# A state-space block with an expert block on one core: four kinds of scratch arrays in memory, laid out with the partition outermost

## The chip, the cores and the metric

The kernel runs on one core of a Trainium2 chip. The core has TensorE (PE in the rows), VectorE (DVE), ScalarE (ACT), GpSimd (POOL) and SyncE (SP), which run side by side and meet at semaphores, and 16 DMA engines that move data between the on-chip memory of 128 partitions and the large memory. The metric is the device time of the whole kernel in microseconds (us), as the median of several runs. Lower is better.

## The reference

The input x has 4 sequences of 1024 tokens with 128 features. First a selective state-space block:

```
xn = layernorm(x);  xi, z = split(xn @ W_in)          # 256 channels each
u  = silu(causal_conv4(xi));  dt, B, C = split(u @ W_xproj)   # 8, 64, 64 wide
delta = softplus(dt @ W_dt + b_dt);  A = -exp(A_log)
for t:  h = h * exp(delta_t * A) + (delta_t * u_t) * B_t;   y_t = h . C_t    # 256 x 64 states
x = layernorm(x + x + (y + u * D) * silu(z) @ W_out)
```

then four layers with four experts each (router, top 2 of 4, layernorm, gelu between two matrices of 128x512 and 512x128), a residual and a last layernorm.

## The kernel before

The kernel has three stages.

**The front** (to about 195 us) computes everything of the state-space block that does not depend on the state. It works on 8 items, k = 0 to 7: item k is half a sequence pair, that is 512 tokens (TT) of one of the two sequences (bb = k % 2) of index it = k // 2. For each item PE, ACT and DVE make u, the gate silu(z) (called sz), C, delta, delta*u and B. Delta, delta*u and B are then split into bf16 parts (the value, its rounding rest, and the rest of that), so that products of parts give fp32 accuracy; six pairs of parts (PAIRS) are used, and for each pair one copy of the delta part, the delta*u part and the B part is stored. All of it goes to scratch arrays in the large memory: `dl_d` (delta, six copies), `du_d` (delta*u, six), `b_d` (B, six), `u_d` and `sz_d` (u and the gate, fp32) and `c_d` (C).

**The scan** (about 170 to 1300 us) works on chunks of 64 tokens (TC); a chunk of a sequence pair is two blocks of 128 channels (kk = 0, 1), 64 blocks in all. A block needs the rows of its chunk in another arrangement than the front made them: `load_args` reads `dl_d` with 8 DMAs of 24 KB into `rhs_d[kk]`, `load_products` reads `b_d` with one DMA of 192 KB and `du_d` with 8 of 24 KB into `Bst[kk]` and `rhs_u[kk]`, `load_c` reads `c_d`, and `load_post` reads `u_d` and `sz_d`. PE multiplies them (L1227 the arguments of the exponential, L1240 the products delta*u*B), ACT takes them out of PSUM (L977 with the exponential, L989), DVE runs the recurrence (`tensor_tensor_scan`, L1596, eight a block), and PE sums the states with C (L1257).

**The experts** (about 1300 us to the end) run on PE above all (L1360, L1372).

All stores of the front and all loads of the scan are issued by SP, one after another in program order. In the front its loop over k does, in this order: load the input of item k + 3 (L516); store u and sz of item k (L593, waits for `a_sz`, `a_u`); in the last item (LAST, k = 7) `load_products(0, 0, 0)` for the first block, once POOL has cleared `rhs_u[0]` (`clear_u[0]`); store the first parts of item k - 1 (`store_part(k - 1, 0)`, L524 and L526, three pairs, waits for `a_p0`); store C (L606, `a_bc`); in the last item `load_args(0, 0, 1)`, `load_products(0, 0, 1)` and `load_c(0, 0)`, each behind its clearing; store the other parts of item k - 1 (three pairs, `a_p1`, `a_p2`); store B of item k (L620, six DMAs, `a_blo`). Behind the loop it stores the parts of item 7, waits until every row has landed and goes on to the loads of the scan. In item 4 it also issues `load_args(0, 0, 0)`.

Buffers overlap in the on-chip memory, so clearings and waits tie the stages together. POOL clears `rhs_u[0]` (L772) when u and sz of item 6 have landed (`a_stored[0]`), `rhs_d[1]` (L775) when those of item 7 have (`a_stored[1]`), then `rhs_u[1]` (L779), and only behind these makes the last parts of B (L782, L784) and sets the first states (L797). In the scan's first block DVE runs one scan, then the remainders of item 7 (L1469, L1471), then the rest; POOL makes the last part of item 7 (L759). The second block's states lie where parts of the odd items lay, so its first scan waits for all stores of these (`a_rows[1]`).

In the arrays before, the partition of the source was not the outermost index. A partition of the on-chip source holds 2 x 512 values of delta in one piece, but in `dl_d` the two halves of the channels lay 128 rows apart, so that each DMA wrote runs of 1 KB; in `du_d` each of the four token tiles gave runs of 512 bytes, in `b_d` runs of 256 bytes, in `u_d` and `sz_d` runs of 2 KB.

Of the kernel before, what the change touches and what calls it, by code (L numbers as in the profile page):

```python
# [11 lines left out]
P = 128  # L12
HALVES = DI // P
BP = B // 2
TC = 64
# [30 lines left out]
def build(nc, x, vecs, chan, taps, a_log, ident, w_in, w_xproj, w_dt, w_out,  # L46
# [7 lines left out]

    dl_d = nc.dram_tensor("dl_d", (NIT, 2, PAIRS, DI, TT), bf16).ap()
    du_d = nc.dram_tensor("du_d", (NIT, 2, PAIRS, TT, DI), bf16).ap()
    b_d = nc.dram_tensor("b_d", (NIT, TT, 2, PAIRS, 2 * N), bf16).ap()
    a_d = nc.dram_tensor("a_d", (DI, RW, 2 * N), bf16).ap()
    c_d = nc.dram_tensor("c_d", (NIT, 2, N, TT), fp32).ap()
    x1_d = nc.dram_tensor("x1_d", (NCH, P, H), fp32).ap()  # L60
    u_d = nc.dram_tensor("u_d", (NIT, 2, DI, TT), fp32).ap()
    sz_d = nc.dram_tensor("sz_d", (NIT, 2, DI, TT), fp32).ap()

    ctx = ExitStack()
    with ctx:
# [445 lines left out]
        def _(sp):  # L511
# [7 lines left out]
            def store_part(k, w):  # L519
                it, bb = k // 2, k % 2  # L520
                sp.wait_ge((a_p0, a_p1, a_p2)[w], k + 1)
                for p in [p for p in range(PAIRS) if X_PART[p] == w]:
                    src = part[bb][w]
                    sp.dma_start(dl_d[it, bb, p].rearrange("(h p) t -> p h t", p=P),  # L524
                                 src[:, 0].rearrange("p (h t) -> p h t", t=TT)).then_inc(a_rows[bb], 16)
                    sp.dma_start(du_d[it, bb, p].rearrange("(k p) d -> p k d", p=P),  # L526
                                 src[:, 1].rearrange("p (k d) -> p k d", d=DI)).then_inc(a_rows[bb], 16)

# [18 lines left out]
            def load_products(c, pair, kk):  # L547

                it, o = pair * 2 + c // CPT, c % CPT * NOCT
                sp.dma_start(Bst[kk][0:ROWS], b_d[it].rearrange("(o e) b p n -> (e b p) o n", e=OCT)  # L550
                             [:, bass.ds(o, NOCT), :]).then_inc(du_in[kk], 16)
                src = du_d[it].rearrange("b p (o e) (k d) -> e k (b p) o d", e=OCT, d=DB)
                for e in range(OCT):
                    sp.dma_start(rhs_u[kk][RW * e:RW * e + RW, :, e, :], src[e, kk, :, bass.ds(o, NOCT), :]
                                 ).then_inc(du_in[kk], 16)

            def load_args(c, pair, kk):

                it, t = pair * 2 + c // CPT, c % CPT * TC
                src = dl_d[it].rearrange("b p (k g i) t -> k i (b p) g t", k=NBLK, i=GI)  # L560
                for i in range(GI):
                    sp.dma_start(rhs_d[kk][RW * i:RW * i + RW, :, i, :], src[kk, i, :, :, bass.ds(t, TC)]
                                 ).then_inc(dl_in[kk], 16)
# [6 lines left out]
            def load_post(c, pair, usz, xres, landed):  # L570

                it, t = pair * 2 + c // CPT, c % CPT * TC
                for i, dram in enumerate((u_d, sz_d)):
                    for h in range(HALVES):
                        sp.dma_start(usz[:, i, h, :, :], dram[it, :, h * P:(h + 1) * P, bass.ds(t, TC)]
                                     .rearrange("b p t -> p b t")).then_inc(landed, 16)
# [9 lines left out]
            for k in range(ITEMS):  # L586
# [5 lines left out]
                for dram, s in ((u_d, u_s), (sz_d, sz_s)):  # L592
                    sp.dma_start(dram[it, bb].rearrange("(h p) t -> p h t", p=P), s[bb]).then_inc(a_stored[bb], 16)  # L593
                if k == 4:
# [24 lines left out]
                for p in range(PAIRS):  # L619
                    sp.dma_start(b_d[it, :, bb, p, :].rearrange("(k p) n -> p k n", p=P),  # L620
                                 b_part[bb][W_PART[p]].rearrange("p k b n -> p k (b n)")).then_inc(a_rows[bb], 16)
# [1301 lines left out]
```

## Time and profile before

| | us |
|---|---|
| median of 3 runs | 2205.91 (2204.47 to 2206.34) |
| the profiled execution | 2200.88 |
| its span, first to last instruction | 2199.3 |
| PE busy | 2125.6 (97%) |
| DVE busy | 1821.8 (83%) |
| ACT busy | 1620.9 (74%) |
| POOL busy | 944.9 (43%) |

The profiled execution took 1.6 us more than its span, and 5.0 us less than the median of the runs. Busy shares are means over the three stages, which have different limits, so they are to be read stage by stage: in slices of time for all engines, then in windows, then instruction by instruction where a stage gives way to the next. The times at which SP issued a DMA stand in its own timeline, and the share and the GB/s of the 16 DMA engines stand in the windows.

### The profile page before, as it was taken

What the parts mean: (1) busy time and instruction counts of PE and PEld (TensorE: products, weight loads), DVE (VectorE), ACT (ScalarE), POOL (GpSimd) and SP (SyncE); (2) the same over time, 40 slices, a digit from 0 to 9 for tenths busy, and PEclk for the clock granted to TensorE, in tenths of its full rate; (3) what the DMA queues carried; (4) which work ended last, traced back from release to release, by engine and by line L of the source; (5) the groups of instructions that cost most, each with busy time, mean ns of one, the idle gap of its engine ahead of it and who ended that gap; (6) DMA issues with size and microseconds to landing.
All of it is one profiled execution on the core that took longest, in us unless ns stands there. A gap on an engine that the chain in (4) does not pass through costs nothing.

```text
span 2199.3 us, 50866 instructions
## 1 busy us (share of the span) xinstructions
PE 2125.6 (97%) x17080; PEld 1267.3 (58%) x17080; DVE 1821.8 (83%) x2689; ACT 1620.9 (74%) x2288; POOL 944.9 (43%) x454
## 2 busy tenths in 40 slices
PE   7968999999999999999999998999999999999998
PEld 3432333333333333333333336899999999999997
DVE  6878999999999999999999997666555566656775
ACT  5878999999999999999999995445455454544453
POOL 3124344444444444444444344544444444444542
PEclk9977999999999999999999999999999999999999
DMA  5995222222212121212222235000100010000000
GB/s 167 283 285 145 47 42 49 43 48 42 47 41 48 40 49 40 49 40 48 42 45 45 43 86 151 1 0 0 39 1 0 0 39 1 0 1 3 13 10 15
DMA packets 354957, 114.93 MB, mean 52 GB/s; under 512 B 283000, under 2 KB 345600, under 8 KB 354624
## 3 DMA queue, kind: packets, MB, share of 16 engines
q1 hardware_dynamic: 350416, 110.92, 20.3%
q10 hardware_dynamic: 4464, 3.02, 0.4%
q8 instruction: 44, 0.72, 0.1%
q14 instruction: 33, 0.27, 0.0%
HBM read 67.98 MB, written 45.88 MB: 52 GB/s over the span
## 4 chain that ended last, share of the span: by engine, by line
PE 57%; DVE 14%; issue 13%; ACT 9%; SPq 6%; POOL 1%; DMA 0%; DVEq 0%; ACTq 0%; POOLq 0%
PE PS L1372 20%; PE PS L1360 16%; DVE arena L1596 12%; PE PS L1257 9%; ACT behind L989 7%; PE PS L1240 5%; PE PS L1227 4%; SPq L524 2%; SPq L526 1%; SPq L620 1%; ACT behind L977 1%; PE PS L1269 1%; PE PS L1271 1%; PE PS L1339 1%; PE PS L1348 0%
## 5 line engine op out<-in xcount | busy, mean ns | idle before, releaser
L1596 DVE TENSOR_TENSOR_SCAN arena<-behind 128x1040 f32<-128x1040 f32 x512 | 1145.0, 2300 | 19.3 <-ACT behind L989 16.6
L1117 ACT ACTIVATE arena<-PS,arena 128x512 f32<-128x512 f32 x512 | 344.6, 688 | 402.5 <-PE PS L1360 401.9
L977 ACT ACTIVATE behind<-PS 128x1024 f32<-128x1024 f32 x512 | 527.0, 1029 | 84.9 <-PE PS L1227 42.3
L1257 PE MATMUL PS<-arena 128*32 128x128 f32 x8192 | 566.0, 406 | 0.0
L989 ACT ACTIVATE behind<-PS 128x1024 f32<-128x1024 f32 (+2 forms) x640 | 547.1, 878 | 22.8 <-PE PS L1240 16.4
L1372 PEld LDWEIGHTS PS<-arena 128*128 128x128 f32 x4096 | 473.3, 192 | 7.6
L1372 PE MATMUL PS<-arena 128*128 128x128 f32 x4096 | 473.7, 275 | 0.0
L797 POOL COPY behind<-carry 128x64 f32<-128x64 f32 x128 | 235.5, 1840 | 478.0 <-DVE arena L1596 337.9
L1257 PEld LDWEIGHTS PS<-arena 128*32 128x32 f32 x8192 | 235.0, 119 | 287.5 <-issue 212.2
L1360 PE MATMUL PS<-parts_xh,parts_w 128*128 128x512 f32 x1536 | 381.3, 400 | 9.0 <-ACT arena L1117 6.2
L1240 PE MATMUL PS<-arena 96*128 96x512 bf16 x1024 | 314.1, 389 | 40.6 <-DMA arena<-du_d 17.8
L1744 DVE SCALAR_TENSOR_TENSOR arena<-PS,arena 128x128 f32 (+1 forms) x508 | 142.9, 344 | 253.3 <-PE PS L1372 252.2
L1360 PEld LDWEIGHTS PS<-parts_xh,parts_w 128*128 128x128 f32 x1536 | 282.5, 190 | 67.6 <-ACT arena L1117 10.3
L1227 PE MATMUL PS<-arena,Ast 96*128 96x512 bf16 x1024 | 314.2, 389 | 2.5 <-ACT behind L977 2.2
L1240 PEld LDWEIGHTS PS<-arena 96*128 96x128 bf16 x1024 | 68.8, 98 | 241.1 <-ACT behind L989 203.1
L1227 PEld LDWEIGHTS PS<-arena,Ast 96*128 96x128 bf16 x1024 | 58.8, 98 | 229.4 <-ACT behind L977 177.9
L844 POOL TENSOR_TENSOR arena<-euler,arena 128x16 f32<-128x16 f32 x32 | 92.6, 2894 | 163.6 <-DVE arena L1685 163.5
L852 POOL TENSOR_TENSOR arena<-arena 128x2048 f32<-128x2048 f32 x32 | 145.8, 4555 | 12.3 <-POOL arena L714 12.3
L861 POOL TENSOR_TENSOR arena<-arena 128x2048 f32<-128x2048 f32 x32 | 115.6, 3612 | 78.3 <-DVE arena L1715 78.3
L714 POOL TENSOR_TENSOR arena<-arena,neg_half 128x4 f32<-128x4 f32 (+1 forms) x50 | 51.1, 1021 | 225.6 <-DVE arena L1434 225.5
L811 POOL COPY arena<-arena 64x64 f32<-64x64 f32 x64 | 128.4, 2006 | 11.8 <-POOL behind L797 9.7
L723 POOL TENSOR_TENSOR arena<-arena,eps_s 128x1 f32<-128x1 f32 x32 | 60.4, 1889 | 150.2 <-DVE arena L1569 150.2
(140 smaller groups left out, 1425.9 us busy)
## 6 DMA issues: line engine op xcount, KB each, us to landing
dl_d<-arena SPq DMA_DIRECT2D x48, 256.0 KB, 3.5
du_d<-arena SPq DMA_DIRECT2D x48, 256.0 KB, 3.5
arena<-dl_d SPq DMA_DIRECT2D x512, 24.0 KB
arena<-b_d SPq DMA_DIRECT2D x64, 192.0 KB
arena<-du_d SPq DMA_DIRECT2D x512, 24.0 KB
b_d<-arena SPq DMA_DIRECT2D x48, 128.0 KB, 2.8
u_d<-behind SPq DMA_DIRECT2D x8, 512.0 KB, 4.0
sz_d<-arena SPq DMA_DIRECT2D x8, 512.0 KB, 4.9
```

Of the source, the lines that this page charges most:

```text
L797: nc.gpsimd.tensor_copy(seg(dB[:, G_])[:, :, 0], carry[:, pair, d:d + GD]).then_inc(slot_ready, 1)
L852: nc.gpsimd.tensor_tensor(scored, X[:, bass.ds(g * GT, GT), :].unsqueeze(2).broadcast_to([P, GT, E, H]), rw_s[:, bass.ds(l, 1)].broadcast_ ...
L977: nc.scalar.activation(seg(dA[:, half])[:, :, 1:], PS[:, 0:2, :].rearrange("p j (i t) -> p (j i) t", t=TC), ACT.Exp).then_inc(exp_done, 1)
L989: nc.scalar.activation(seg(dB[:, G_])[:, lo:hi, 1 + 2 * OCT * r:1 + 2 * OCT * (r + 1)], PS[:, 2:4, :].rearrange("p o (t d) -> p d (o t)", ...
L1117: nc.scalar.activation(hT[:, e % 2, c], PS[:, HIDDEN[(GT * e + c) % 3], :], ACT.Gelu, bias=bias1[:, lp, e * GT + c:e * GT + c + 1]).then_i ...
L1227: last = nc.tensor.matmul(PS[:, j, :], Ast[0:ROWS, kk * (DB // GI) + 2 * q + j, :], rhs_d[kk][0:ROWS, 2 * q + j].rearrange("r i t -> r (i ...
L1240: last = nc.tensor.matmul(PS[:, 2 + oct_ % 2, :], Bst[kk][0:ROWS, oct_, :], rhs_u[kk][0:ROWS, oct_, :, G_ * GD:(G_ + 1) * GD], start=True, ...
L1257: last = nc.tensor.matmul(PS[32 * j:32 * j + 32, 4 + kk, 0:DB], cd[:, pair, j, 32 * i:32 * i + 32], seg(hb[kk])[:, :, 1 + 16 * j + i], sta ...
L1360: last = nc.tensor.matmul(PS[:, HIDDEN[(GT * e + c) % 3], :], w1p[:, lp, part_w, e, c * P:(c + 1) * P], xhT[:, gp, part_x], start=(part_w ...
L1372: last = nc.tensor.matmul(PS[:, y_bank(n, e, s), s * P:(s + 1) * P], hT[:, e % 2, c, s * P:(s + 1) * P], w2_s[lp][:, e * GT + c], start=(c ...
L1596: nc.vector.tensor_tensor_scan(hb[kk][:, q * QD * SEG:(q + 1) * QD * SEG], dA[:, q % 2], dB[:, G_, lo:lo + QD * SEG], 0.0, ALU.mult, ALU.a ...
L1744: last = nc.vector.scalar_tensor_tensor(at(X, g, s), PS[:, Y_BANK[e], s * P:(s + 1) * P], comb[:, gp, s * E + e:s * E + e + 1], at(X, g, s ...
```

## The change

Five arrays get another order of indices in memory: `dl_d` from (channel, token) to (partition, half, token), `du_d` from (token, channel) to (partition, tile, channel), `b_d` from token outermost to partition outermost with the tile inside, and `u_d` and `sz_d` from (channel, token) to (partition, half, token). With that, what one partition of the source holds for one DMA lies in one run in memory: 2 KB in `dl_d` and `du_d`, 1 KB in `b_d`, 4 KB in `u_d` and `sz_d`. The loads of the scan are rewritten to find the same values; the runs that they read stay as long as they were (128 bytes of `dl_d`, 256 bytes of `du_d`, `b_d`, `u_d` and `sz_d`), at other distances. Which DMAs are issued, in which order, behind which waits, and how many bytes they move is unchanged.

```diff
@@ -52,14 +52,14 @@
     ACT = mybir.ActivationFunctionType
     AX = mybir.AxisListType
 
-    dl_d = nc.dram_tensor("dl_d", (NIT, 2, PAIRS, DI, TT), bf16).ap()
-    du_d = nc.dram_tensor("du_d", (NIT, 2, PAIRS, TT, DI), bf16).ap()
-    b_d = nc.dram_tensor("b_d", (NIT, TT, 2, PAIRS, 2 * N), bf16).ap()
+    dl_d = nc.dram_tensor("dl_d", (NIT, 2, PAIRS, P, HALVES, TT), bf16).ap()
+    du_d = nc.dram_tensor("du_d", (NIT, 2, PAIRS, P, TT // P, DI), bf16).ap()
+    b_d = nc.dram_tensor("b_d", (NIT, P, 2, PAIRS, TT // P, 2 * N), bf16).ap()
     a_d = nc.dram_tensor("a_d", (DI, RW, 2 * N), bf16).ap()
     c_d = nc.dram_tensor("c_d", (NIT, 2, N, TT), fp32).ap()
     x1_d = nc.dram_tensor("x1_d", (NCH, P, H), fp32).ap()
-    u_d = nc.dram_tensor("u_d", (NIT, 2, DI, TT), fp32).ap()
-    sz_d = nc.dram_tensor("sz_d", (NIT, 2, DI, TT), fp32).ap()
+    u_d = nc.dram_tensor("u_d", (NIT, 2, P, HALVES, TT), fp32).ap()
+    sz_d = nc.dram_tensor("sz_d", (NIT, 2, P, HALVES, TT), fp32).ap()
 
     ctx = ExitStack()
     with ctx:
@@ -521,10 +521,8 @@
                 sp.wait_ge((a_p0, a_p1, a_p2)[w], k + 1)
                 for p in [p for p in range(PAIRS) if X_PART[p] == w]:
                     src = part[bb][w]
-                    sp.dma_start(dl_d[it, bb, p].rearrange("(h p) t -> p h t", p=P),
-                                 src[:, 0].rearrange("p (h t) -> p h t", t=TT)).then_inc(a_rows[bb], 16)
-                    sp.dma_start(du_d[it, bb, p].rearrange("(k p) d -> p k d", p=P),
-                                 src[:, 1].rearrange("p (k d) -> p k d", d=DI)).then_inc(a_rows[bb], 16)
+                    sp.dma_start(dl_d[it, bb, p].rearrange("p h t -> p (h t)"), src[:, 0]).then_inc(a_rows[bb], 16)
+                    sp.dma_start(du_d[it, bb, p].rearrange("p k d -> p (k d)"), src[:, 1]).then_inc(a_rows[bb], 16)
 
             load_x(0)
             sp.dma_start(taps_s.rearrange("p t d -> p (t d)"), taps).then_inc(taps_in, 16)
@@ -546,18 +544,17 @@
 
             def load_products(c, pair, kk):
 
-                it, o = pair * 2 + c // CPT, c % CPT * NOCT
-                sp.dma_start(Bst[kk][0:ROWS], b_d[it].rearrange("(o e) b p n -> (e b p) o n", e=OCT)
-                             [:, bass.ds(o, NOCT), :]).then_inc(du_in[kk], 16)
-                src = du_d[it].rearrange("b p (o e) (k d) -> e k (b p) o d", e=OCT, d=DB)
+                it, tile, half = pair * 2 + c // CPT, c % CPT // 2, c % 2
+                sp.dma_start(Bst[kk][0:ROWS], b_d[it].rearrange("(m o e) b r k n -> m k (e b r) o n", m=2, e=OCT)
+                             [half, tile]).then_inc(du_in[kk], 16)
+                src = du_d[it].rearrange("b r (m o e) q (k d) -> m q e k (b r) o d", m=2, e=OCT, d=DB)[half, tile]
                 for e in range(OCT):
-                    sp.dma_start(rhs_u[kk][RW * e:RW * e + RW, :, e, :], src[e, kk, :, bass.ds(o, NOCT), :]
-                                 ).then_inc(du_in[kk], 16)
+                    sp.dma_start(rhs_u[kk][RW * e:RW * e + RW, :, e, :], src[e, kk]).then_inc(du_in[kk], 16)
 
             def load_args(c, pair, kk):
 
                 it, t = pair * 2 + c // CPT, c % CPT * TC
-                src = dl_d[it].rearrange("b p (k g i) t -> k i (b p) g t", k=NBLK, i=GI)
+                src = dl_d[it].rearrange("b r (g i) k t -> k i (b r) g t", i=GI)
                 for i in range(GI):
                     sp.dma_start(rhs_d[kk][RW * i:RW * i + RW, :, i, :], src[kk, i, :, :, bass.ds(t, TC)]
                                  ).then_inc(dl_in[kk], 16)
@@ -572,7 +569,7 @@
                 it, t = pair * 2 + c // CPT, c % CPT * TC
                 for i, dram in enumerate((u_d, sz_d)):
                     for h in range(HALVES):
-                        sp.dma_start(usz[:, i, h, :, :], dram[it, :, h * P:(h + 1) * P, bass.ds(t, TC)]
+                        sp.dma_start(usz[:, i, h, :, :], dram[it, :, :, h, bass.ds(t, TC)]
                                      .rearrange("b p t -> p b t")).then_inc(landed, 16)
                 sp.dma_start(xres, tokens(x, c, pair)).then_inc(landed, 16)
 
@@ -590,7 +587,7 @@
                 sp.wait_ge(a_sz, k + 1)
                 sp.wait_ge(a_u, k + 1)
                 for dram, s in ((u_d, u_s), (sz_d, sz_s)):
-                    sp.dma_start(dram[it, bb].rearrange("(h p) t -> p h t", p=P), s[bb]).then_inc(a_stored[bb], 16)
+                    sp.dma_start(dram[it, bb], s[bb]).then_inc(a_stored[bb], 16)
                 if k == 4:
 
                     sp.wait_ge(clear_d[0], 1)
@@ -617,7 +614,7 @@
                     store_part(k - 1, 2)
                 sp.wait_ge(a_blo, k + 1)
                 for p in range(PAIRS):
-                    sp.dma_start(b_d[it, :, bb, p, :].rearrange("(k p) n -> p k n", p=P),
+                    sp.dma_start(b_d[it, :, bb, p],
                                  b_part[bb][W_PART[p]].rearrange("p k b n -> p k (b n)")).then_inc(a_rows[bb], 16)
             for w in range(PARTS):
                 store_part(LAST, w)
```

On SP, the whole loop stands in the same order. This is the end of item 6 and the beginning of item 7 before (what is written, what is read, its shape, and what it waits for):

```order
L524 DMA dl_d<-arena 128x2x512 [waits a_p2]
L526 DMA du_d<-arena 128x4x256
L620 DMA b_d<-arena 128x4x128 [waits a_blo]
L620 DMA b_d<-arena 128x4x128 x5
L593 DMA u_d<-behind 128x2x512 [waits a_u,a_sz]
L593 DMA sz_d<-arena 128x2x512
L550 DMA arena<-b_d 96x8x128 [waits clear_u0]
L554 DMA arena<-du_d 12x8x128 x8
```

and this is the same place of the changed kernel:

```order
L524 DMA dl_d<-arena 128x1024 [waits a_p2]
L525 DMA du_d<-arena 128x1024
L617 DMA b_d<-arena 128x512 [waits a_blo]
L617 DMA b_d<-arena 128x512 x5
L590 DMA u_d<-behind 128x1024 [waits a_u,a_sz]
L590 DMA sz_d<-arena 128x1024
L548 DMA arena<-b_d 96x8x128 [waits clear_u0]
L552 DMA arena<-du_d 12x8x128 x8
```

No instruction has moved; the stores have lost their middle index, since each partition's part is now one run, and the loads have the shapes that they had. PE, ACT, DVE and POOL have the same instructions in the same order.

## Rows read from the trace of the kernel before

**Rows 1.** The page: the span in 40 slices, about 55 us each.

```profile
PEclk9977999999999999999999999999999999999999
DMA  5995222222212121212222235000100010000000
```

**Rows 2.** Windows of 20 us: length, busy of each engine, clock, DMA share, GB/s.

```profile
120.00:140.00 20.00, 19.40 (x68) 9.40 (x67) 16.39 (x18) 18.00 (x20) 2.10 (x4) 1.00 0.98 304
140.00:160.00 20.00, 4.39 (x21) 2.49 (x19) 12.82 (x13) 10.46 (x10) 4.34 (x2) 0.57 0.97 282
200.00:220.00 20.00, 19.57 (x181) 6.23 (x182) 20.00 (x10) 18.22 (x22) 8.27 (x4) 1.00 0.23 43
```

**Rows 3.** Timeline of PE: start, length, the convolution of two items in a row.

```profile
109.43 7.14 PE L1150 MATMUL PS<-arena,behind 128*128 128x512 f32 x16
125.94 7.14 PE L1150 MATMUL PS<-arena,behind 128*128 128x512 f32 x16
```

**Rows 4.** Timeline of SP: u of items 2, 3 and 7, B of item 6, the first loads.

```profile
62.88 0.51 SPq L593 DMA_DIRECT2D u_d<-behind  x1
...
80.74 0.48 SPq L593 DMA_DIRECT2D u_d<-behind  x1
...
149.25 4.09 SPq L620 DMA_DIRECT2D b_d<-arena  x6
153.44 0.51 SPq L593 DMA_DIRECT2D u_d<-behind  x1
154.00 0.53 SPq L593 DMA_DIRECT2D sz_d<-arena  x1
154.57 1.19 SPq L550 DMA_DIRECT2D arena<-b_d  x1
155.80 4.41 SPq L554 DMA_DIRECT2D arena<-du_d  x8
```

**Rows 5.** Windows of PE with DMA share and GB/s, one item's stores.

```profile
64.00:67.00 3.00, 3.00 (x9) 1.00 1.04 376
67.00:77.00 10.00, 9.40 (x43) 1.00 1.03 322
...
102.00:103.00 1.00, 1.00 (x6) 1.00 1.05 408
135.00:137.00 2.00, 2.00 (x5) 1.00 0.88 215
```

**Rows 6.** The line of the delta stores: shortest, median, longest issue on SP, ns.

```profile
L524 SPq DMA_DIRECT2D dl_d<-arena x48: 406/810/1291, 45.1 to 190.9; - x48
```

**Rows 7.** Timelines of PE, ACT and DVE where the scan begins.

```profile
143.33 1.06 PE L1227 MATMUL PS<-arena,Ast 96*128 96x512 bf16 x2
162.17 1.03 PE L1240 MATMUL PS<-arena 96*128 96x512 bf16 x2 [17.77 <-DMA arena<-du_d]
...
150.47 1.02 ACT L977 ACTIVATE behind<-PS 128x1024 f32<-128x1024 f32 x1
163.30 1.06 ACT L989 ACTIVATE behind<-PS 128x1024 f32<-128x1024 f32 x1 [11.81 <-PE PS L1240]
165.48 1.06 ACT L989 ACTIVATE behind<-PS 128x1024 f32<-128x1024 f32 x1 [1.12 <-PE PS L1240]
...
170.32 2.33 DVE L1596 TENSOR_TENSOR_SCAN arena<-behind 128x1040 f32<-128x1040 f32 x1 [16.60 <-ACT behind L989]
```

**Rows 8.** Timeline of POOL there: B parts, the three clearings, the last part.

```profile
139.02 0.64 POOL L784 TENSOR_TENSOR arena<-behind,arena 128x256 bf16<-128x256 f32 x1
141.31 3.51 POOL L772 MEMSET arena<- 128x4096 f32 x1 [1.65 <-DMA sz_d<-arena]
159.17 3.51 POOL L775 MEMSET arena<- 128x4096 f32 x1 [14.36 <-DMA sz_d<-arena]
...
177.22 4.07 POOL L759 TENSOR_TENSOR arena<-arena 128x2048 bf16<-128x2048 f32 x1 [9.54 <-ACT arena L930]
```

**Rows 9.** Timeline of DVE where the second block begins, and SP's next load.

```profile
192.25 2.29 DVE L1596 TENSOR_TENSOR_SCAN arena<-behind 128x1040 f32<-128x1040 f32 x1
195.62 22.27 DVE L1596 TENSOR_TENSOR_SCAN arena<-behind 128x1040 f32<-128x1040 f32 x10 [1.08 <-DMA du_d<-arena]
...
196.03 3.41 SPq L554 DMA_DIRECT2D arena<-du_d  x8
```

**Rows 10.** Timeline of SP in the scan, and the window of the scan from 205 us.

```profile
239.47 4.12 SPq L554 DMA_DIRECT2D arena<-du_d  x8
244.60 3.71 SPq L562 DMA_DIRECT2D arena<-dl_d  x8
...
205.00:640.00 435.00, 429.46 (x4049) 157.48 (x4052) 435.00 (x227) 401.61 (x516) 192.06 (x95) 1.00 0.22 45
```

## The prediction

> **What bounds the kernel now.** Start with the page's slices [rows 1]: the DMA engines are busy at nine tenths in the second and third slice, and nowhere near that in the scan or the experts. The clock of TensorE is down in the third and fourth. So the change, which touches stores of the front alone, must pay there or nowhere. The windows of 20 us [rows 2] say which engine is short in the front. Up to 140 us PE is busy 19.4 of 20 us while the DMA engines stand at 0.98: both are full. From 140 to 160 us PE has only 4.4 us of work, its clock is at 0.57, and the DMA engines are still at 0.97: the arithmetic of the front is over and the core waits for stores. From 200 us the scan runs, DVE is busy without a gap and DMA is at 0.23.
>
> Two paces have to be told apart. PE takes an item every 125.94 - 109.43 = 16.5 us [rows 3]. SP, which issues the stores, takes one every 80.74 - 62.88 = 17.9 us [rows 4]. SP is the slower, and it falls behind: B of item 6 was ready when POOL's L784 ended at 139.66 [rows 8], and SP issued it at 149.25 [rows 4], 9.6 us late. That SP is held by the DMA engines and not by its own work is seen in the issue of a delta store: 406 ns at its shortest, 810 ns in the median [rows 6], and 256 KB in 810 ns is 324 GB/s, just what the engines move in that stretch (322, [rows 5]).
>
> What this lateness costs stands in the hand-over. PE had the first arguments of the scan at 144.4 and then waited 17.8 us for the du_d load, to 162.17; ACT was free at 151.49 (L977) and got the first products at 163.30; DVE's first scan started at 170.32 [rows 7]. The second block began at 195.62, of which 1.08 us is a wait for the last stores [rows 9]. From there to the end of the scan DVE has no gap [rows 10], and the experts follow on PE: whatever is gained up to 195.62 is kept, nothing later is gained.
>
> **The stores, priced.** An item stores 1.05 MB of u and sz, 3.15 MB of delta and delta*u, 0.79 MB of B, 0.13 MB of C and loads 0.26 MB of x. The rate depends on the run [rows 5]: 408 GB/s with the 2 KB runs of u and sz (376 in the three us that also hold the change-over), 322 with delta and delta*u mixed, runs of 1 KB and 512 bytes, and 215 with B's 256 bytes. That gives 1.05/0.408 = 2.6, 3.28/0.322 = 10.2, 0.79/0.215 = 3.7 and about 0.9 us for x, 17.4 us in all, against the 17.9 measured. So the pieces explain the pace.
>
> After the change delta and delta*u have the runs that u and sz have now: 3.15/0.408 = 7.7 us, and C 0.4. For B with 1 KB no row stands alone: it lies between 322 and 408, so 1.9 to 2.4 us, and I take 2.1, since the 322 is held down by the 512-byte half. U and sz with 4 KB have no row either; I leave them at 408, where they can only be underrated a little. The sum is 2.6 + 8.1 + 2.1 + 0.9 = 13.7 us, below the 16.5 us of PE. The `load_args` in item 4 costs SP some 4 us once; with 2.8 us of spare time an item that is gone two items later. SP then waits for the engines in every item, not they for it.
>
> By the Trainium skill, "DMA: Bandwidth & Descriptors", Why small descriptors are slow, each packet carries about 3 cycles on top of one per 32 bytes; if 2 KB runs give 408, that would make 1 KB runs 392 and B 2.0 us, but 256-byte runs 311, where the trace shows 215 [rows 5], so the trace falls short of it at the short end.
>
> **The hand-over, followed.** SP's order is fixed, so the last item starts with B of item 6, ready at 139.66 [rows 8]. Six issues of about 0.45 us (a delta store that nothing held took 0.41, [rows 6]) end at 142.4; u and sz of item 7 (two issues of 0.5) end at 143.4. The clearing of rhs_u[0] took 3.51 us and had waited 1.65 us for a store [rows 8]; that wait goes, so it runs 139.7 to 143.2 and SP need not wait for it. The loads of B and delta*u took 1.19 + 4.41 = 5.6 us behind a full queue [rows 4]; the same kind of load behind nothing took 3.4 + 0.4 [rows 9]. So they end between 147.2 and 149.0. PE started 162.17 - 160.21 = 2.0 us after the last issue, and ACT 1.1 us after PE [rows 7]: products are ready for ACT between 150.3 and 152.1, and ACT itself is free at 151.5. I take 151.6 for ACT's first L989, against 163.30: **11.7 us earlier**. What would be late next is ACT, not the load; the two are within a microsecond of each other.
>
> From ACT's L989 to DVE's first scan nothing depends on stores: four rounds of PE and ACT of 2.18 us each (163.30 to 165.48, [rows 7]), so the first scan comes at 170.32 - 11.7 = 158.6. POOL must have its clearings and B parts done by then. The second clearing follows the landing of sz of item 7, issued at 142.9; before, it started 159.17 - 154.00 = 5.2 us after that issue, so it starts at 148.1 at the latest, the third ends at 155.1, and B's parts and the state slots (1.6 us) end before 157: hidden, with 1.6 us to spare. The clearings now run beside DVE's work on item 7; L772 already ran beside it and took the same 3.51 us, so I charge nothing.
>
> **The second block.** It needs all stores of the odd items. From about 148.2 SP still has 24 stores of delta and delta*u, C, the loads of the block (3.7 + 4.4 + 0.4), and B: 24 x 0.64 + 0.5 + 8.5 + 2.6 = 27.0 us, issue over at 175.2, landed 3.5 us later at 178.7. DVE finishes the first block at 192.25 + 2.29 - 11.7 = 182.8, so the wait of 1.08 us [rows 9] goes too, with 4 us to spare. POOL's L759 hangs on ACT [rows 8] and shifts with it. **Sum: 11.7 + 1.1 = 12.8 us** off the profiled execution, 2200.9 to 2188.1. That execution stands 5.0 us below the median of the runs, and the saving carries over unchanged: 2205.9 - 12.8 = **2193.1 us**.
>
> The loads of the scan read runs of the same length at other distances. A block's du and dl loads take SP 4.12 + 3.71 us [rows 10] of its 17.8 us, at a DMA share of 0.22; the loads are made a block ahead, and no wait of PE for them stands in the trace beyond the first. I cost this at nothing.
>
> **Rivals.** *Only B gets faster.* Delta and delta*u might be held at 322 GB/s by something other than the run (the on-chip side, the many DMAs in turn). For it: no row shows 2 KB runs from bf16 parts. Against it: the same queue moved 408 as soon as u and sz came. An item would take 2.6 + 10.2 + 2.1 + 0.9 = 15.8 us; with item 4's extra loads and a last interval of 14.8 us, SP reaches B of item 6 some 3 us late, ACT starts at about 154.5, and the 24 last stores take 0.81 us each, so that their landing, at 186, sets the second block: 9.6 us gained, 2196.3 us. The Trainium skill, same page, Specifications, puts the least transfer for line rate at 512 bytes; by that rule delta and delta*u would already be there, and this is the case it gives, though 322 against 408 in the rows speaks against it.
>
> *The clock comes back sooner.* PE idled from 144.4 to 162.2 and its clock fell to half in that stretch; with some 5 us of idleness the products might run at full clock, which would shorten the three rounds by 0.4 us each (an L1227 or L1240 pair takes 1.03 us at half clock and about 0.6 at full). Against it: the clock was already down at 0.57 over a window whose first three us were full of PE work. 1.3 us more: 2191.8.
>
> *The change does not act.* If SP's pace hung on the bytes and not on the runs, its times would stay and so would 2205.9. The three rates [rows 5] at the same full share speak against it.
>
> *Slower: the scan's loads lengthen.* Rows of B that a load takes side by side lay 256 bytes apart in memory and now lie 1 KB apart. SP has in a chunk of two blocks (35.7 us) about 20 us of such issues (twice the 8 us of [rows 10] and the small ones). Below 1.8 times their length nothing is seen; above it SP sets the pace. At twice, a chunk takes 3.6 us longer, and over 31 chunks the kernel takes 112 us longer less the 12.8: 2305. The runs are as long as before, and this is why I hold it for unlikely.
>
> **How the numbers follow.** The forecast has 0.62, only B faster 0.16, the clock 0.10, no action 0.08, slower 0.04. The first three lie between 2191.8 and 2196.3; the bounds of the load (1.7 us), of B's rate and of the run-to-run spread of 2 us on either side widen that to 2190 to 2199, which leaves out the last two. About 0.2% (4.4 us) is what a measurement of this kernel can tell from no change. Faster by more than that: the first three and a little less, for a hand-over that is met later than I think, 0.88; within: 0.08; slower: 0.04.
>
> **What would show it.** SP's u stores should follow the items at 16.5 us and not 17.9; the issue of a delta store should fall from 0.81 to about 0.64 us or less; the windows of the front should show a DMA share near 0.8; B of item 6 should be issued near 139.7, ACT's first L989 near 151.6, DVE's first scan near 158.6, the second block near 182.8 with no wait for a store. PE may still sit at half clock between 143 and 185. If SP is on time and the first products still come after 153, the loads behind the stores are the step that failed; if the second block waits, the last stores are.

## The result, and the profile after

The changed kernel takes 2190.69 us (median of 6 runs, 2188.92 to 2195.77), the one before 2205.03 us (6 runs, 2203.81 to 2206.34). The ratio is 0.9945 with a 95% interval of 0.9933 to 0.9956, which is 9.7 to 14.8 us, or 12.1 us in the middle. The profiled executions differ by 11.0 us: 2200.88 and 2189.90, with spans of 2199.3 and 2188.3.

The page of the changed kernel, in the same 40 slices as [rows 1], here with the packets of all queues:

```profile
PEclk9988999999999999999999999999999999999999
DMA  5784222121212122222222234000100010000000
...
DMA packets 309901, 114.93 MB, mean 53 GB/s; under 512 B 258424, under 2 KB 290304, under 8 KB 309568
```

The same bytes go in 45,056 fewer packets (354,957 before), and the DMA engines are no longer at nine tenths in the second and third slice. The windows show the rates (length, PE busy, clock, DMA share, GB/s): one us within the stores of u and the gate of item 2 (4 KB runs), eight us of the delta and delta*u stores of item 1 with C among them, one us of these eight, and two us of the B stores of item 2.

```profile
65.00:66.00 1.00, 1.00 (x4) 1.00 1.04 426
67.00:75.00 8.00, 7.97 (x35) 1.00 1.04 377
68.00:69.00 1.00, 1.00 (x4) 1.00 1.06 406
77.00:79.00 2.00, 2.00 (x5) 1.00 0.78 263
```

Delta, delta*u and C now move at 377 GB/s in the mean, where they moved at 322 [rows 5]: single microseconds of delta and delta*u show 373 to 410, and the one that holds C only 242. B moves at 263 for 215, at a share of only 0.78. SP's timeline at the end of the front, to be held against [rows 4]:

```profile
126.42 3.29 SPq L617 DMA_DIRECT2D b_d<-arena  x6
...
140.55 3.33 SPq L617 DMA_DIRECT2D b_d<-arena  x6
143.97 0.40 SPq L590 DMA_DIRECT2D u_d<-behind  x1
144.41 0.45 SPq L590 DMA_DIRECT2D sz_d<-arena  x1
144.90 0.78 SPq L548 DMA_DIRECT2D arena<-b_d  x1
145.73 4.41 SPq L552 DMA_DIRECT2D arena<-du_d  x8
...
154.31 6.60 SPq L559 DMA_DIRECT2D arena<-dl_d  x8
```

B of item 6 was ready at 139.96, when POOL's L781 ended, and was issued 0.6 us later, not 9.6 us. The first products follow, on PE, ACT, DVE and POOL (against [rows 7] and [rows 8]):

```profile
151.77 1.03 PE L1237 MATMUL PS<-arena 96*128 96x512 bf16 x2 [6.75 <-DMA arena<-du_d]
...
150.78 1.02 ACT L974 ACTIVATE behind<-PS 128x1024 f32<-128x1024 f32 x1
152.90 1.06 ACT L986 ACTIVATE behind<-PS 128x1024 f32<-128x1024 f32 x1 [1.10 <-PE PS L1237]
...
159.92 2.33 DVE L1593 TENSOR_TENSOR_SCAN arena<-behind 128x1040 f32<-128x1040 f32 x1 [5.88 <-ACT behind L986]
...
168.62 33.27 DVE L1593 TENSOR_TENSOR_SCAN arena<-behind 128x1040 f32<-128x1040 f32 x14 [1.59 <-ACT behind L974]
...
139.33 0.63 POOL L781 TENSOR_TENSOR arena<-behind,arena 128x256 bf16<-128x256 f32 x1
148.61 3.51 POOL L772 MEMSET arena<- 128x4096 f32 x1 [5.19 <-DMA sz_d<-arena]
```

PE waits 6.75 us for the first load, where it waited 17.77. ACT's wait has shrunk from 11.8 to 1.1 us and DVE's from 16.6 to 5.9. The row of 14 scans holds the rest of the first block and the start of the second with nothing between: the wait of 1.08 us for stores [rows 9] is gone. Before, the last six scans of the first block took 15.5 us, and from 168.62 that gives 184.1 for the second block, 11.5 us earlier than 195.62:

```profile
179.02 15.52 DVE L1596 TENSOR_TENSOR_SCAN arena<-behind 128x1040 f32<-128x1040 f32 x6 [1.59 <-ACT behind L977]
```

That no store was waited for was close. SP issued the last store of item 7 at 180.17 and went on at 183.38, when the last had landed, 0.7 us before the second block began:

```profile
180.17 0.65 SPq L525 DMA_DIRECT2D du_d<-arena  x1
183.38 0.34 SPq L548 DMA_DIRECT2D arena<-b_d  x1
```

One thing was new. The issue of the scan's delta loads on SP, shortest, median and longest in ns, before and after:

```profile
L562 SPq DMA_DIRECT2D arena<-dl_d x512: 298/304/1658, 99.6 to 1293.4; - x171
```

```profile
L559 SPq DMA_DIRECT2D arena<-dl_d x512: 770/773/1872, 96.7 to 1284.9; - x171
```

Each of the 512 loads takes SP two and a half times as long, with the same shape and bytes.

### The profile page after: what moved, and what is told of

Its sections match the earlier page's. It is cut to its first block, busy times and chain, and to the rows that moved or that the text cites. A ratio compares the mean times of both kernels' runs of the same rounds, so it can differ in the third digit from the quotient of the medians.

```text
span 2188.3 us, 50866 instructions
## 1 busy us (share of the span) xinstructions
PE 2126.6 (97%) x17080; PEld 1269.2 (58%) x17080; DVE 1822.1 (83%) x2689; ACT 1620.8 (74%) x2288; POOL 947.7 (43%) x454
## 4 chain that ended last, share of the span: by engine, by line
PE 57%; DVE 15%; issue 13%; ACT 10%; SPq 2%; POOL 1%; DVEq 0%; DMA 0%; ACTq 0%; POOLq 0%
PE PS L1369 20%; PE PS L1357 16%; DVE arena L1593 12%; PE PS L1254 9%; ACT behind L986 7%; PE PS L1237 5%; PE PS L1224 4%; ACT behind L974 1%; PE PS L1266 1%; PE PS L1268 1%; PE PS L1336 1%; SPq L525 1%; SPq L617 1%; SPq L524 1%; PE PS L1345 0%
## 5 line engine op out<-in xcount | busy, mean ns | idle before, releaser
L974 ACT ACTIVATE behind<-PS 128x1024 f32<-128x1024 f32 x512 | 527.1, 1029 | 84.0 <-PE PS L1224 44.7
L1741 DVE SCALAR_TENSOR_TENSOR arena<-PS,arena 128x128 f32 (+1 forms) x508 | 142.9, 344 | 253.5 <-PE PS L1369 252.3
L808 POOL COPY arena<-arena 64x64 f32<-64x64 f32 x64 | 129.2, 2019 | 11.8 <-POOL behind L794 9.7
```

The source lines that it names most:

```text
L974: nc.scalar.activation(seg(dA[:, half])[:, :, 1:], PS[:, 0:2, :].rearrange("p j (i t) -> p (j i) t", t=TC), ACT.Exp).then_inc(exp_done, 1)
L1741: last = nc.vector.scalar_tensor_tensor(at(X, g, s), PS[:, Y_BANK[e], s * P:(s + 1) * P], comb[:, gp, s * E + e:s * E + e + 1], at(X, g, s ...
```

## The experiments

All were compared with runs of the kernel before on the same chip. Two measures of the trace are used beside the time, since they leave out what differs between executions elsewhere: how late SP issues B of item 6 after POOL has made it, and how long it is from that moment to the first scan of the second block (the hand-over). Where the profile has no row of its own for that scan, because no gap stands before it, it is 15.5 us after the row of the third scan of the first block.

In every trace the time from the start of the second block to the start of the last scan is 1133.2 to 1133.8 us, so the scan keeps its pace with each of these layouts. From there to the end the traces take 870.4 to 875.3 us, whatever the edit. That is why a microsecond won in the hand-over can be missing from the time.

| kernel | ratio (95%) | SP late with B of item 6, us | hand-over, us |
|---|---|---|---|
| before | | 9.6 | 56.0 |
| the same again | 1.0003 (0.9993 to 1.0013) | 8.8 | 54.9 |
| only B | 0.9977 (0.9967 to 0.9986) | 5.4 | 49.9 |
| only delta*u | 0.9965 (0.9952 to 0.9977) | 2.6 | 47.6 |
| only delta | 1.0007 (0.9998 to 1.0017) | 9.6 | 57.7 |
| only delta, padded | 0.9989 (0.9980 to 0.9999) | 7.5 | 52.7 |
| delta and delta*u | 0.9965 (0.9953 to 0.9978) | 3.5 | 48.6 |
| all, with gaps in memory | 1.0026 (1.0014 to 1.0037) | 11.3 | 59.6 |
| all (the change) | 0.9945 (0.9933 to 0.9956) | 0.6 | 44.2 |
| all, once more | 0.9943 (0.9921 to 0.9965) | 0.1 | 43.7 |
| all, delta padded | 0.9944 (0.9928 to 0.9961) | 0.0 | 43.0 |
| all, B of item 6 moved | 0.9946 (0.9929 to 0.9962) | moved | 43.0 |
| all, padded and moved | 0.9943 (0.9922 to 0.9964) | moved | 43.0 |
| all, B in four DMAs | 0.9947 (0.9931 to 0.9963) | 0.0 | 43.0 |

**The same kernel again.** No edit.

> The kernel before, once more, so that it can be seen how far two traces and two series of runs of one kernel lie apart. The traces of before and after differ by 11.0 us, the medians by 14.3 us. If the difference of 3 us is run-to-run spread, this kernel's median lies within 2 us of the one before and its profiled execution within 5 us; its hand-over should show the same numbers (SP 9.6 us late with B of item 6, first products on ACT 12.8 us after it was ready for them, second block near 195.6).

Measured: 2202.18 us for 2201.95 of the kernel before beside it. Its median held, but its profiled span was 2202.6 where the first had 2199.3, although the second block began at 195.40 and 195.62. The windows of the expert stage show where the 3.3 us lie (clock in the third column), first the kernel before, then this one:

```profile
1540.00:1560.00 20.00, 20.00 (x128) 0.91 0.00 1
1740.00:1760.00 20.00, 20.00 (x152) 1.00 0.00 1
```

```profile
1540.00:1560.00 20.00, 20.00 (x115) 0.83 0.00 0
1740.00:1760.00 20.00, 20.00 (x139) 0.91 0.00 1
```

PE is busy throughout, and in stretches of some 3.4 or 6.7 us its granted clock is the lower of its two levels (1.2 for 2.4 GHz). In these two windows the second execution spent some 6.6 us more at that level, which is 3.3 us more for the same work, since PE is the limit there. So two executions of one kernel differ by 3 us, and that the medians differed by 14.3 us and the traces by 11.0 needs no other cause.

**Only B.**

```diff
-    b_d = nc.dram_tensor("b_d", (NIT, TT, 2, PAIRS, 2 * N), bf16).ap()
+    b_d = nc.dram_tensor("b_d", (NIT, P, 2, PAIRS, TT // P, 2 * N), bf16).ap()
```

with its store and its load as in the change.

> Only b_d has the new layout (runs of 1 KB for 256 bytes), the other four arrays are as before. After the full change six B stores took SP about 3.3 us for 4.1. Theory (SP's lateness adds up item by item while an item costs it more than the 16.5 us of PE): some 0.8 us less in each of items 1 to 6, SP about 5 us late where it was 9.6, the second block and the time 4.5 to 5.5 us earlier. Rival (every microsecond saved on the DMA engines counts alike): B's share of 0.8 in 3.1 us an item, times the 11 us of the whole change, 2.8 us.

Measured: 2197.60 us for 2201.95, 5.1 us less by the ratio, hand-over 5 to 6 us shorter, SP 5.4 us late. The theory had 4.5 to 5.5, the proportional rival 2.8. The saving does add up item by item: B of items 2 to 6 was issued 0.4, 1.7, 6.3, 7.1 and 9.6 us after it was ready in the kernel before, and 0, 0.2, 3.8, 4.1 and 5.4 us here. These numbers show one thing more: 4.6 of the 9.6 us come up in item 4 alone, where SP also issues the eight delta loads (5.38 us). No run takes them out of item 4. For item 6 here:

```profile
146.85 3.61 SPq L621 DMA_DIRECT2D b_d<-arena  x6
```

```profile
140.79 0.64 POOL L785 TENSOR_TENSOR arena<-behind,arena 128x256 bf16<-128x256 f32 x1
```

**Only delta*u.**

```diff
-    du_d = nc.dram_tensor("du_d", (NIT, 2, PAIRS, TT, DI), bf16).ap()
+    du_d = nc.dram_tensor("du_d", (NIT, 2, PAIRS, P, TT // P, DI), bf16).ap()
```

with its store and its loads as in the change.

> Only du_d has the new layout (2 KB for 512 bytes). Theory: delta and delta*u together saved 2.2 us an item after the change; the larger part should be du's, about 1.4 us, since its runs were the shorter, so that six items give 7 to 8 us. If the run length above 512 bytes does not matter, as the rule of 512 bytes has it, nothing is gained: 0 us.

Measured: 7.7 us less by the ratio, as the theory had it. From 512 bytes to 2 KB is worth more than from 256 bytes to 1 KB, since delta*u has twice the bytes of B. A rule by which 512 bytes are enough is out for these stores.

**Only delta.**

```diff
-    dl_d = nc.dram_tensor("dl_d", (NIT, 2, PAIRS, DI, TT), bf16).ap()
+    dl_d = nc.dram_tensor("dl_d", (NIT, 2, PAIRS, P, HALVES, TT), bf16).ap()
```

with its store and its loads as in the change.

> Only dl_d has the new layout (2 KB for 1 KB). The stores should save 0.7 to 0.9 us an item, 4 to 5 us by item 6; against this the eight delta loads of a block, whose issue took 0.30 us each before and 0.77 us after the change, cost SP 3.8 us more in item 4. Theory: 1 to 3 us gained in all. If the longer issue has another cause than the layout of dl_d, it stays at 0.30 us here and the gain is 4 to 5 us.

Measured: 1.5 us more by the ratio, an interval that holds no change, where 1 to 3 us less were expected; the theory had the sign of both terms and the wrong balance. The eight loads in item 4 stand behind a full queue and had taken 5.38 us before, not eight times 0.30. They took 7.24 us here, so that they cost 1.9 us more and not 3.8; those in item 7 took 6.61 us for 3.96. SP had stored u of item 4 at 96.54, 1.9 us sooner than before (98.43), and was through the loads at the same time as before (105.0), so in item 4 they ate just what the stores had saved. SP was as late as before with B of item 6, and the second block waited longer for the last stores than it did [rows 9], because the slower loads stand ahead of them. The loads of item 4 before, and here:

```profile
99.64 5.38 SPq L562 DMA_DIRECT2D arena<-dl_d  x8
```

```profile
97.71 7.24 SPq L561 DMA_DIRECT2D arena<-dl_d  x8
```

```profile
196.42 4.54 DVE L1595 TENSOR_TENSOR_SCAN arena<-behind 128x1040 f32<-128x1040 f32 x2 [2.69 <-DMA du_d<-arena]
```

**All, with gaps in memory.** Every array has its partition outermost, but the pieces of a partition are apart, and an unused piece keeps partitions apart as well:

```diff
-    du_d = nc.dram_tensor("du_d", (NIT, 2, PAIRS, P, TT // P, DI), bf16).ap()
+    du_d = nc.dram_tensor("du_d", (NIT, 2, PAIRS, P, TT // P + 1, DI + 128), bf16).ap()
```

and the other four likewise; every store and load names the used part only.

> The five arrays with the partition outermost as in the change, but with unused room between the pieces of a partition, so that every store writes runs as short as before (1 KB, 512 bytes, 256 bytes, 2 KB). Theory (the run length is what counts): no gain at all, and the delta loads still issue at 0.77 us each, which cost 1 to 2 us when dl_d alone was changed: 0 to 3 us slower than before. Rival (it is the order of the addresses, not the length of a run): the gain of the whole change, 10 to 14 us.

Measured: 2207.70 us for 2202.74, 5.7 us more by the ratio. The stores move as before: 337 GB/s in the window from 67 to 77 us, where the kernel before has 322, and the six B stores of item 6 take 4.14 us for 4.09. So the gain hangs on the run length, and not on having the partition outermost. The loss is larger than the 0 to 3 us expected; the hand-over is 3.6 us longer than before, as SP is 11.3 us late and the second block waits for stores:

```profile
202.45 13.40 DVE L1593 TENSOR_TENSOR_SCAN arena<-behind 128x1040 f32<-128x1040 f32 x6 [3.01 <-DMA du_d<-arena]
```

and POOL made B of item 6 at 142.9, 3.2 us later than before, in an execution whose windows show a lower clock (0.83) between 20 and 40 us. Whether all five us come from the delta loads is therefore not shown.

**All, with delta padded.**

```diff
-    dl_d = nc.dram_tensor("dl_d", (NIT, 2, PAIRS, P, HALVES, TT), bf16).ap()
+    dl_d = nc.dram_tensor("dl_d", (NIT, 2, PAIRS, P + GI, HALVES, TT), bf16).ap()
...
-                src = dl_d[it].rearrange("b r (g i) k t -> k i (b r) g t", i=GI)
+                src = dl_d[it][:, :, 0:P].rearrange("b r (g i) k t -> k i (b r) g t", i=GI)
```

> The whole change, with dl_d padded to 136 rows for each pair. In the changed kernel the address steps of a delta load happen to fit so that its two outer indices on the memory side fall together into one of 192 rows, while the on-chip side keeps 12 x 16; the padding prevents that. Theory: this is why the issue of such a load takes 0.77 us; it falls back to 0.30 us. On the time it should be worth little, 0 to 1 us, since SP is only 0.6 us late with B of item 6 after the change. Rival: the longer issue comes from the larger distance between rows; it stays at 0.77 us, as the distance is the same here.

Measured, first the issue of the loads here, then in the kernel with gaps, where the two outer indices fall together as in the change:

```profile
L559 SPq DMA_DIRECT2D arena<-dl_d x512: 298/304/1233, 96.1 to 1280.6; - x171
```

```profile
L559 SPq DMA_DIRECT2D arena<-dl_d x512: 770/773/1324, 102.7 to 1303.1; - x171
```

The distance between rows is the same as in the change, so the distance is not the cause. By the shapes in the kernels, the memory side of such a load is 12 x 16 rows of 64 values. In the changed kernel 16 steps of 8192 values are just one pair's array, so that the two indices can be written as one of 192; before (16 steps of 4096) and with the padding they can't. The on-chip side is 12 x 16 in all of them. In all seven traces of kernels where the two indices fit together the issue takes 0.77 us, and in the seven where they don't, 0.30. The distance from one pair to the next is no cause either: it is the same 131072 values before (0.30 us) and after (0.77 us). That the compiler does join the two indices, and that SP then spends its time on the unequal sides, is inferred; no view shows the pattern as compiled. On the time it is worth what was expected, nothing that the runs can tell (0.9944 for 0.9943 and 0.9945); the hand-over is 0.7 to 1.2 us shorter.

**Only delta, padded.** The same padding and store, and nothing else of the change.

> Only dl_d has the new layout, padded to 136 rows, so that its stores write 2 KB and its loads issue at 0.30 us. With dl_d alone unpadded the kernel was as fast as before within the measurement (second block at 57.7 us for 55 to 56) and SP was as late with B of item 6 (9.6 us). Theory: the longer load issues had eaten what the stores saved; now SP is 3 to 5 us less late, the second block begins at 51 to 53 us, 2.5 to 5 us faster than before. Rival (the rule of 512 bytes: 1 KB and 2 KB runs are worth the same): no gain.

Measured: 2.4 us less by the ratio, interval 0.2 to 4.4, and the hand-over 2 to 3 us shorter. SP is 7.5 us late: 2.1 us less than in the first trace of the kernel before and 1.3 less than in its second, not 3 to 5, so that delta's stores save 0.2 to 0.35 us an item. So the longer load issues had eaten the gain of delta alone. Delta*u took 6.2 to 7.0 us off the same lateness, three times as much and more: most of what was missing at 322 GB/s [rows 5] was the 512-byte runs' doing.

**Delta and delta*u.** The two edits above together, unpadded.

> dl_d and du_d have the new layout, B, u and the gate the old one. Theory of lateness: du alone left SP 2.6 us late with B of item 6, delta's shorter stores take that away, its longer load issues in item 4 give 3 to 4 us back, B's stores cost 0.8 us more an item than in the full change: 7 to 9.5 us faster than before, 2 to 4 us slower than the full change. If the parts simply added up (5.1 for B in the full change), it would be 11 or 14.3 less 5.1: 6 to 9 us; the two agree here, so this run is to see whether delta is worth anything next to du (du alone: 7.7 us).

Measured: 7.7 us less by the ratio, the same as delta*u alone. The hand-over is even 1.0 us longer than with delta*u alone. Next to delta*u, delta brings nothing as long as its loads issue slowly.

**All, with B of item 6 moved.** In the last item the six B stores of item 6 come behind the first loads:

```diff
                 if k == LAST:
                     sp.wait_ge(clear_u[0], 1)
                     load_products(0, 0, 0)
+                    sp.wait_ge(a_blo, k)
+                    store_b(k - 1)
...
-                sp.wait_ge(a_blo, k + 1)
+                if k != LAST - 1:
+                    sp.wait_ge(a_blo, k + 1)
+                    store_b(k)
```

> The whole change, and in the last item B of item 6 is stored behind the first loads and not ahead of u and the gate of item 7. After the change PE still waits 6.75 us for the first delta*u load and ACT 1.1 us for PE. Theory: the loads now start when POOL's clearing ends, some 1.4 us sooner, ACT gets its first products as soon as it is free: 1.0 to 1.4 us faster than the changed kernel, no more, since ACT is the next limit. If something else holds the first products: no difference.

Measured: the loads started 3.5 us after B of item 6 was ready and not 4.9 (142.92 for 144.90, in an execution whose front was 0.5 us earlier). ACT had its first products as soon as it was free, and the hand-over was 43.0 us, 0.7 to 1.2 us shorter; the time, 2190.32 us, can't be told from that of the change.

**All, once more, and padded and moved together.**

> The changed kernel once more, so that the three others are compared on one chip with it and with the one before. From B of item 6 being ready to the start of the second block of the scan it took 44.2 us, before 54.9 and 56.0 us in two traces of one kernel. Theory: 44 us again, within 1 us, and 11 to 14 us faster than before.

> The whole change with dl_d padded (delta loads issue at 0.30 us) and with B of item 6 stored behind the first loads. Alone, each brought the second block to 43.0 us after B of item 6 was ready, 1.2 us sooner than the changed kernel. Theory: both remove the same thing, SP's last lateness ahead of the first products, and ACT is the next limit, so together they give 43 us again and the same time as either, 1 us below the changed kernel. Rival: the two add up, 41.8 us and 2.4 us.

Measured: the change again 2189.15 us and 43.7 us of hand-over; both edits together 2190.18 us and 43.0 us, the same as either. There the products were ready before ACT was (PE began on them at 148.55, ACT finished its other work at 151.7). That is what a next limit looks like: SP has nothing left to give here, and ACT, which has its own work until 151 to 152 us, sets the first products.

**All, with B in four DMAs.** In place of the loop over six stores:

```diff
+                for w, ps in ((0, (0, 4, 3)), (1, (1, 5, 3)), (0, (5, 6, 1)), (2, (2, 3, 1))):
+                    rows = len(range(*ps))
+                    sp.dma_start(b_d[it, :, bb, ps[0]:ps[1]:ps[2]].rearrange("p r k n -> p r (k n)"),
+                                 b_part[bb][w].rearrange("p k b n -> p (k b n)").unsqueeze(1)
+                                 .broadcast_to([P, rows, 8 * N])).then_inc(a_rows[bb], 16)
```

> The whole change, and the six B stores of an item are put into four DMAs (two of them write two pairs from one source part), with the same bytes in the same runs of 1 KB. After the change B was the one store with a DMA share well under 1 (0.77, 263 GB/s), each issue taking SP about 0.46 us for 128 KB. If SP's issue is what holds B, four DMAs take 2 to 2.4 us an item for 2.8 and the rate rises above 300 GB/s; the time gains 0.3 to 1 us. If 1 KB runs of B move at 263 GB/s whatever issues them, the rate stays and nothing is gained.

Measured: where nothing held it, SP issued B in 1.9 to 2.0 us for 2.8. With that B starts and ends earlier, so its windows are others than in the change; these lie within the B stores of items 1, 2 and 3:

```profile
59.00:61.00 2.00, 2.00 (x5) 1.00 1.01 334
76.00:77.00 1.00, 1.00 (x3) 0.50 0.97 342
92.00:94.00 2.00, 2.00 (x5) 1.00 1.02 337
```

The change had 261 to 263 GB/s at a share of 0.78 in such windows. So in the changed kernel SP's issue and not the 1 KB run held B. The 1 KB runs themselves fill the engines at 334 to 342 GB/s, still less than the 373 to 410 of 2 KB runs. The hand-over was 43.0 us once more and the time 2190.69 us: nothing gained, as ACT is the next limit.

## Why the prediction was right

**What bounds the kernel now: right.** Only the front's stores and the hand-over changed. SP's pace was set by the DMA engines and through them by the length of a run; the kernel with gaps shows that last point: with the new order of indices and the old run lengths nothing is gained. The median issue of a delta store fell from 810 to 639 ns, as forecast.

**The stores: right in the mechanism, B mis-sized.** Delta and delta*u were put at 408 GB/s and C at 0.4 us, 8.1 us together; at the 377 GB/s measured for the three it is 8.7, above all because C drags. B was put between 322 and 408 and moved at 263: 3.0 us an item and not 2.1. The bounds were taken from other arrays' runs of similar length, but B comes in DMAs of 128 KB, and each takes SP some 0.46 us; the rate of a store can't exceed its bytes by its issue time, 128 KB in 0.46 us being 285 GB/s. That bound stood in the rows for any DMA (shortest issue 406 ns, [rows 6]). From B of item 5 to B of item 6, with no wait, SP took 140.55 - 126.42 = 14.1 us, where the forecast's terms without x give 12.8: 0.9 of the difference is B's, 0.6 that of delta, delta*u and C. U and the gate with 4 KB runs went at 426 for 408, worth 0.1 us an item; no run has them alone. The forecast's estimate of 392 GB/s for 1 KB runs (390 by its own working) is not met either, since B in four DMAs shows 334 to 342. The pace of 14.1 us was still below PE's pace, so SP caught up, and the error cost only its part at the hand-over.

**The hand-over: 11.7 us forecast, 10.4 measured.** ACT's first products came at 152.90 and not at 151.6. Of the 1.3 us, 0.6 is the time from B being ready to its issue, for which the forecast had none, 0.6 the six issues (3.33 us for 2.7); this execution's front also ran 0.3 us later (ACT's L974 at 150.78 for 150.47), and the rest of the chain gave 0.2 back. The loads took 5.2 us, within the 3.8 to 5.6 forecast. The 0.6 us come from item 4: its loads took SP 7.1 us, where the forecast has some 4 (5.38 even before), and B was 3.3 us late there, 1.2 in item 5 and 0.6 in item 6. With delta padded it is 0.9 and then nothing. The order of the limits was right: moving B or padding delta brought 0.7 to 1.2 us and no more together than apart, since ACT comes next. POOL's second clearing, put at 148.1 at the latest, started at 148.61, later than that bound since u and sz themselves went out later, and was hidden as forecast.

**The second block: right in the result, wrong in the margin.** No wait for stores, 184.1 for 182.8; the 1.08 us gained are as much as the first trace had, the second trace of the same kernel had 0.42. But the forecast had the last store landed at 178.7, with 4 us to spare, and it landed at 183.4, with 0.7, later than the 182.8 that the forecast has for the block itself. SP was 2.0 us later at the start of this stretch than assumed, the delta loads took 6.6 us for 3.7, and B 3.3 for 2.6. With delta padded the last store landed at 178.2 and the block began at 182.3.

**The scan's loads: wrong, and cheap.** They were put at nothing, as their runs kept their length. The step that failed is that only runs and distances were looked at, and not how the indices of the two sides fall together. The delta loads' issue went from 0.30 to 0.77 us, 3.8 us for a block's eight. That is the slower rival's mechanism in a small form: it was to decide from 1.8 times SP's 20 us a chunk, and SP now needs about 28 us of 35.7 (an estimate: twice 3.8 more), 1.4 times the 20, so that the scan doesn't show it. It did show where SP was short: in item 4 (1.9 us) and in item 7 (2.7 us), where it made the whole of delta's part worthless, and it took the 0.7 to 1.2 us of hand-over that the padding gives back.

**The rivals.** Only B faster: delta*u alone gave 7.7 us, so it is out, and with it the rule of 512 bytes from the Trainium skill, "DMA: Bandwidth & Descriptors", Specifications, as far as these stores are concerned. The clock coming back: PE was at half clock at the first products, as before (0.50 in the windows from 143 to 163 us); in both traces it had fallen by 143 us, with PE still busy, and not in PE's wait, as the prediction has it. From ACT's first products to DVE's first scan it took 7.02 us in both traces, so those 1.3 us weren't there. No action: out. Slower: out, though its price has a slip, since twice 20 us is 4.3 us over 35.7 and not 3.6, 133 us in 31 chunks and not 112.

**The sum.** 12.8 us were forecast; the traces differ by 11.0, the ratio gives 12.1 with an interval of 9.7 to 14.8. The last scan started 11.4 us earlier (1317.5 for 1328.9), which is the size that the steps explain; from 2205.9 it would give 2194.5. That the median fell on 2190.7, 2.4 us below the forecast and 0.7 inside the range's lower end, no step explains: single executions of one kernel differ by 3 us and more with the clock in the expert stage. That part is chance.

## What to carry to other kernels

Price a queue of stores by run length and by issue separately, item by item, and compare the sum with the pace of the engine that feeds it: below that pace a saving is worth nothing, above it it is worth itself times the number of items. Near that pace parts don't add up: in the hand-over B alone gave 5.0 to 6.1 us, delta*u alone 7.3 to 8.4 and padded delta alone 2.2 to 3.3, together 14.5 us at least, and all with the padding 11.9 to 13.0. The times don't tell it: B, delta*u and unpadded delta alone add up to 11.3 us, against 9.7 to 14.8 for the change. When a layout is changed for the sake of the stores, look at the loads' access patterns on both sides and at what each load costs the engine that issues it: two indices that happen to fit together on one side only made each load cost SP 0.47 us more, and a padding of eight rows undid it.

## What the runs showed of the hardware that was not expected

The issue of one DMA from SP with 192 rows of 128 bytes took 0.30 us when both sides had indices of 12 x 16, and 0.77 us when those of the memory side could be joined to one of 192 and those of the on-chip side not; the bytes, the runs and the distances between rows were the same (padded and not, 512 loads in each of the traces). How the compiler wrote the pattern isn't shown.

At a full DMA share, stores from on-chip memory moved at 426 GB/s with runs of 4 KB, at 373 to 410 with 2 KB and at 334 to 342 with 1 KB; with 256 bytes they moved at 215, at a share of 0.88. The six B stores of 128 KB, at 0.46 us of SP each, left the engines at a share of 0.78 and 263 GB/s.

The granted clock fell for some 3.4 or 6.7 us at a time to its lower level in the expert stage and at times in the front, with PE busy all the while, at other places from one execution of the same kernel to the next: 0.91 and 1.00 in the two windows from 1540 and from 1740 us in one, 0.83 and 0.91 in the other, 3.3 us of span apart. What sets these stretches isn't shown.
